# A four-layer graph kernel: two of every sixteen attention units turned on VectorE and carried through memory, a new order of SyncE's loads, and three held chunks in the last layer

## The reference, cut to what matters

```
x = _layernorm(x + _L0_gnn_ref(x, adj, ...))   # agg = adj @ x, then a GRU cell
x = _layernorm(x + _L1_gnn_ref(x, adj, ...))   # D^-1/2 (adj + I) D^-1/2 (x @ W) + b
x = _layernorm(x + _L2_gnn_ref(x, adj, ...))   # 4-head attention over the edges of adj
x = _layernorm(x + _L3_gnn_ref(x, adj, ...))   # hyperbolic layer: support_t = adj @ xt

# the attention
attn  = jnp.einsum('nhc,mhc->hnm', q, k) / np.float32(np.sqrt(C))
e     = jnp.where(mask[None], 0.0, jnp.exp(neg - m))
alpha = e / denom
out   = jnp.einsum('hnm,mhc->hnc', alpha, v)
out   = beta * x_r + (1.0 - beta) * out

# the end of the hyperbolic layer
h  = proj(expmap0(support_t, C_IN), C_IN)
xt = jax.nn.relu(logmap0(h, C_IN))
h  = proj(expmap0(xt, C_OUT), C_OUT)
```

## Time and profile before

| | |
|---|---|
| median of 3 runs | 1879.82 us |
| the profiled execution, its own time | 1879.74 us |
| its span, first to last instruction | 1877.9 us |
| PE busy | 1809.2 us (96%) |
| DVE busy | 1208.7 us (64%) |
| ACT busy | 1023.2 us (54%) |
| POOL busy | 964.4 us (51%) |
| mean granted TensorE clock | 0.985 |

### The profile page before, as it was taken

How to read it: one execution, slowest core, us unless ns; L and a number is a source line. 1 busy time by engine, 2 the same in 40 slices (tenths; PEclk the granted TensorE clock), 3 DMA queues, 4 the chain that set the end, 5 groups by cost and what they waited for, 6 DMA issues and landing times.

```text
span 1877.9 us, 41628 instructions
## 1 busy us (share of the span) xinstructions
PE 1809.2 (96%) x15504; PEld 1217.3 (65%) x15504; DVE 1208.7 (64%) x2246; ACT 1023.2 (54%) x1640; POOL 964.4 (51%) x1069
## 2 busy tenths in 40 slices
PE   7999999999997999999999999999999999889995
PEld 3444444444444888888888888888888888544442
DVE  4777774122226888888889888988889888201111
ACT  0111111000015888888888988888888889213323
POOL 0111111111126657688688787787887886353323
PEclk9999999999997999999999999999999999999998
DMA  9767767899976232313223232233232220879891
GB/s 376 295 229 260 253 230 243 281 385 386 397 267 201 85 91 69 92 57 98 80 75 91 69 92 90 60 92 90 74 90 72 89 77 30 325 238 322 293 319 41
DMA packets 110303, 328.79 MB, mean 175 GB/s; under 512 B 13104, under 2 KB 31280, under 8 KB 85552
## 3 DMA queue, kind: packets, MB, share of 16 engines
q1 hardware_dynamic: 87552, 285.25, 44.2%
q10 hardware_dynamic: 20016, 32.78, 4.8%
q0 software_dynamic: 2560, 8.39, 1.5%
HBM read 299.11 MB, written 27.26 MB: 174 GB/s over the span
## 4 chain that ended last, share of the span: by engine, by line
PE 48%; issue 8%; POOL 7%; ACT 3%; DVE 2%; DMA 1%; POOLq 0%; SPq 0%; DVEq 0%; ACTq 0%
PE bank L562 21%; PE bank L535 13%; PE bank L576 12%; ACT arena L792 2%; POOL arena L1337 1%; POOL small L1337 1%; POOL arena L1330 1%; PE bank L428 1%; DMA arena<-root_dram 1%; DVE arena L1123 1%; POOL small L1276 1%; POOL small L1511 0%; POOL arena L1519 0%; POOL small L1513 0%; POOL small L1496 0%
## 5 line engine op out<-in xcount | busy, mean ns | idle before, releaser
L562 PE MATMUL bank<-ident,arena 128*128 128x128 f32 x4096 | 539.9, 274 | 5.4 <-ACT arena L792 2.4
L562 PEld LDWEIGHTS bank<-ident,arena 128*128 128x128 f32 x4096 | 477.9, 141 | 82.5 <-DVE arena L1123 7.8
L792 ACT ACTIVATE arena<-arena,small 128x2048 f32<-128x2048 f32 x256 | 512.5, 2002 | 0.1
L428 PE MATMUL bank<-arena,stat_s 128*128 128x512 f32 x1016 | 448.5, 599 | 6.9 <-POOL stat_s L1337 4.9
L804 ACT ACTIVATE arena<-bank 128x512 f32<-128x512 f32 x680 | 382.5, 596 | 125.2 <-PE bank L562 123.0
L535 PE MATMUL bank<-k,parts 128*128 128x512 f32 x1024 | 372.0, 445 | 13.9 <-DVE small L1108 6.9
L428 PEld LDWEIGHTS bank<-arena,stat_s 128*128 128x128 f32 x1016 | 193.4, 193 | 237.1 <-issue 230.0
L1123 DVE COPY arena<-bank 128x512 f32<-128x512 f32 x344 | 236.6, 688 | 72.6 <-PE bank L562 71.4
L1330 POOL TENSOR_SCALAR early<-arena 128x512 bf16<-128x512 f32 x128 | 246.2, 1923 | 71.1 <-DVE small L1108 31.4
L576 PE MATMUL bank<-arena,stat_x 128*32 128x128 f32 x8192 | 276.5, 276 | 0.0
L1330 POOL TENSOR_SCALAR arena<-arena 128x512 bf16<-128x512 f32 x128 | 247.1, 1931 | 41.4 <-DVE small L1108 19.6
(11 more groups left out here) (160 smaller groups left out, 1309.3 us busy)
## 6 DMA issues: line engine op xcount, KB each, us to landing
arena<-adj_cols SPq DMA_DIRECT2D x191, 1024.0 KB, 6.0
arena<-adj SPq DMA_DIRECT2D x256, 256.0 KB, 2.7
k_dram<-arena ACTq DMA_DIRECT2D x32, 256.0 KB, 7.1
q_dram<-arena ACTq DMA_DIRECT2D x32, 256.0 KB, 12.2
k<-k_dram POOLq DMA_DIRECT2D x32, 256.0 KB, 8.8
parts<-q_dram SPq DMA_DIRECT2D x128, 64.0 KB, 2.3
x_dram<-arena ACTq DMA_DIRECT2D x16, 256.0 KB, 3.6
arena<-x_dram ACTq DMA_DIRECT2D x16, 256.0 KB, 5.9
```

The costliest lines, as they stand in the source:

```text
L428: mm_ = pe.matmul(bank[:, to, :], stat[:, jt, :], ring[:, s, j, :], start=(jt == 0), stop=(jt == TILES - 1))
L562: last = pe.transpose(bank[:, b_, h * P:(h + 1) * P], cols[:, st % SETS, h, u * P:(u + 1) * P], ident[:, :])
L792: act.activation(cols[:, s_, h, :], cols[:, s_, h, :], ACT.Exp, bias=shift[:, t % 2, 1, i:i + 1], scale=-1.0, accum_out=blocksum[:, t % 2, ...
```

## The change

It has four parts, and nothing else moves.

1. **Two of 16 units are bounced.** `BOUNCED = {11: 1, 15: 6}`: units 11 and 15 of each group have no transposes on PE, no PSUM bank and no copy. DVE turns them at places 1 and 6 of the group in 32x32 blocks into one buffer, `blocks` (four tiles of `stat_s`). SP stores the buffer to memory (256 KB) and loads it back in four transfers of 64 KB into the unit's slot of `turned`. `attend` waits for these and reads the slot through another pattern. DVE copies 32 of the other 112 units and ACT 80; the tables of places change to match.
2. **SP's order.** For each column n of a chunk, SP now loads the mask of column n+7; then, for even n, it stores both units of group n/2, and for odd n loads both. Queries, residuals and the store of `x3` get fixed places between them.
3. **Three held chunks in layer 3** (`HELD` = 3), so that PE has 21 slots to multiply ahead of `xt`. `turn_x3` and `mobius_product` move back by one slot each.
4. **`hyperbolic`** takes no more logarithms. A closed form, `min(un, artanh(MAX_NORM)) / un`, replaces tanh and two logarithms, most of the small steps move from POOL to DVE, and the squares of `relu` run on DVE beside those on ACT.

```diff
+BOUNCED = {11: 1, 15: 6}
+VECTOR_PLACES = (2, 5, 9, 13)
+MASK_AHEAD = 7
...
+            def store_blocks(g):
+                i = block_turns(g)
+                at, before = i % len(BOUNCED), i // len(BOUNCED)
+                sp.wait_ge(blocks_turned, i + 1)
+                if before:
+                    sp.wait_ge(unit_landed[at], 64 * before)
+                sp.dma_start(bounce_dram[at, :, :], blocks).then_inc(blocks_out[at], 16)
+            def load_unit(g):
+                i = block_turns(g)
+                at, before = i % len(BOUNCED), i // len(BOUNCED)
+                sp.wait_ge(blocks_out[at], 16 * (before + 1))
+                sp.wait_ge(unit_used, g - TURNED + 1)
+                for j in range(4):
+                    sp.dma_start(turned[g % TURNED][j * C:(j + 1) * C, :]...,
+                                 bounce_dram[at, :, j * P:(j + 1) * P]...).then_inc(unit_landed[at], 16)
+            def attention_loads(c):
+                for n in range(COLS):
+                    ahead = c * COLS + n + MASK_AHEAD
+                    if ahead < CHUNKS * COLS:
+                        load_mask(ahead // COLS, ahead % COLS, False)
+                    first_unit = c * UPC + n // 2 * UPS
+                    if n % 2 == 0:
+                        for u in BOUNCED:
+                            store_blocks(first_unit + u)
+                    else:
+                        for u in BOUNCED:
+                            load_unit(first_unit + u)
...
+                if is_bounced(k):
+                    i = block_turns(c * UPC + k)
+                    pe.wait_ge(unit_landed[i % len(BOUNCED)], 64 * (i // len(BOUNCED) + 1))
...
+            def turn_blocks(c, k):
+                st, u = k // UPS, k % UPS
+                i = block_turns(c * UPC + k)
+                dve.wait_ge(exp_ready, (c * SPC + st) * H + H)
+                if i > 0:
+                    dve.wait_ge(blocks_out[(i - 1) % len(BOUNCED)], 16 * ((i - 1) // len(BOUNCED) + 1))
+                dve.transpose(blocks..., cols[:, st % SETS, :, u * P:(u + 1) * P]...).then_inc(blocks_turned, 1)
...
-            product(2, 1, {}, to=4, slots=range(SLOTS - 1))
+            product(2, 1, {0: [lambda: mobius_product(last, 3)]}, to=HELD_BANKS[1], slots=range(SLOTS - 1))
+            product(2, 2, {}, to=HELD_BANKS[2], slots=range(SLOTS - 1))
```

More of the change, by code:

```diff
@@ L97, in __call__, with is_bounced, pe_turns, block_turns @@
         return c * len(self.names) + self.names.index(name) + 1
+def is_bounced(k):
+    return k % UPS in BOUNCED
+PE_UNITS = [k for k in range(UPC) if not is_bounced(k)]
+def pe_turns(g):
+    return g // UPC * len(PE_UNITS) + sum(k < g % UPC for k in PE_UNITS)
+def block_turns(g):
+    return g // UPS * len(BOUNCED) + sum(u < g % UPS for u in BOUNCED)
 class TurnBanks:
@@ L108, in __init__ @@
         for k in range(UPC):
-            self.uses.append(("unit", k))
+            if not is_bounced(k):
+                self.uses.append(("unit", k))
             if k % UPT == OUT_AT:
@@ L138 @@
 LAST_BLOCK_CHUNK = CHUNKS - BLOCK // CHUNK
-BY_VECTOR = [k for k in range(UPC) if (k % 16 in VECTOR_PLACES or k in VECTOR_ALSO) and k not in VECTOR_NOT]
-BY_SCALAR = [k for k in range(UPC) if k not in BY_VECTOR]
+BY_VECTOR = [k for k in PE_UNITS if (k % 16 in VECTOR_PLACES or k in VECTOR_ALSO) and k not in VECTOR_NOT]
+BY_SCALAR = [k for k in PE_UNITS if k not in BY_VECTOR]
 EXP_PLACES = [EXP_MOVED.get(k, k) for k in range(1, UPC, 4)]
@@ L351, in load_queries @@
                                  ).then_inc(q4_landed[t % 2], 16)
[L353 to L358, removed]
-                    if m == 5 and not first:
-                        load_residuals(c - 1)
-                    if m == 15 and not first:
+            def store_blocks(g):
[5 more added lines that the diff above has]
+                sp.dma_start(bounce_dram[at, :, :], blocks).then_inc(blocks_out[at], 16)
@@ L408, in _ @@
+            load_slot(HELD, SLOTS - 1, HELD * (SLOTS - 1) + 1)
+            for c in range(HELD + 1, CHUNKS):
+                for s in range(SLOTS):
+                    load_slot(c, s, (c - 1) * SLOTS + s + 1)
             sp.wait_ge(hyp_out, 16 * CHUNKS)
@@ L612, in attention @@
                         scores(*ahead, False)
-                    turn_unit(c, k, first)
+                    if not is_bounced(k):
+                        turn_unit(c, k, first)
                     if k % UPT == OUT_AT:
@@ L1210, in attention @@
                         below_max(c, k // UPT)
+                    for u, place in BOUNCED.items():
+                        if k % UPS == place:
+                            turn_blocks(c, k - place + u)
                     if k in BY_VECTOR:
```

231 lines of the change are left out of this document (127 added, 104 removed).

## The result

The changed kernel took **2083.17 us** (median of 4 runs, 2078.03 to 2086.09) against 1879.87 for the kernel before (1879.78 to 1882.38, 4 runs): a ratio of 1.108, with an interval of 1.106 to 1.110. It is slower, as forecast, by 203 us and not by 150, and it lies 3 us above my range.

What follows compares the result with a forecast made beforehand. PE was taken to bound the attention. Six chunks +168, chunk 0 -2, chunk 7 +6, its end +3 and layer 3 -23 gave +152 on 1879.74: 2032, stated as 2030 us; range 1930 to 2080.

Steps and rivals of the forecast that it cites:

- 32 us a chunk: PE's waits for bounced unit loads: 5.4, 3.9, 8.7, 4.5, 7.3 us in groups 1, 3, 5, 6, 7; about 0.7 in others.
- Inside the same waits: DVE's second transpose, place 6, held some 6 us in groups 5 and 7 by the first's store, within PE's unit-load waits.
- 25 to 35 us a chunk: Sign: PE idle before the attend (L652) for transfers from bounce_dram, 25 to 35 us, largest at place 15, groups 5 and 7.
- DVE's load: In a chunk: eleven copies fewer, sixteen block transposes at 0.69 us more; 113.2 becomes 116.6 us, 127.7 at the upper bound.
- The tail of layer 3: After layer 3's last turn: y written about 8 us later in place of 13.5, a gain of 5.5 us.
- the clock: Half clock on PE after long waits in the attention: 0 to 8 us lost a chunk, 3.5 taken.
- The saving: PE's transposes of two of 16 units gone: 0.47 us a unit, 7.5 us a chunk, 60 us in all.
- 24.5: Net loss of a held chunk before clock: 32 us of waits less 7.5 saved, about 24.5 us more, 152.5 a chunk.
- my 6: Chunk 7: only groups 0 to 4 wait, about 12 us less 7.5, and a little clock: +6 us.
- Chunk 0: First chunk, without post steps: eight waits of 0.7 us against 7.5 saved, -2 us.
- Layer 3: Gain of 23 us (18 from waits and clock, 5.5 from the tail), less 3 for loads queued behind unit loads.
- my 18: PE in layer 3: its waits of 5.62 and 4.88 us and their clock go, -18 us.

Runs made afterwards that it cites:

- e1: The changed kernel with no unit bounced and the earlier tables of places, everything else kept; 1859.46 us, 0.990 of the kernel before.
- e2: The changed kernel with masks loaded 6 columns ahead in place of 7, both units still bounced; 1921.71 us, 1.020 of the kernel before.
- one unit: The changed kernel with only unit 11 bounced, unit 15 turned by PE again; 2052.57 us, 1.092 of the kernel before.
- e13: e11 with ACT's Moebius tanh four places later, at place 95 instead of 91; 1885.18 us, 1.004 of the kernel before.
- e7: No unit bounced, PE's work as in the kernel before; PE waits 4 times a chunk for two small transfers in a row; 1958.25 us.
- e4: The changed kernel with two block buffers for DVE in chunks 0 to 6, SP's order unchanged; 2065.36 us, 1.100 of the kernel before.
- e5: e2 with each mask load issued behind the stores or unit loads of its iteration; 2073.62 us, 1.103 of the kernel before.
- e9: e2 with unit 11's loads issued ahead of the mask load in odd iterations, unit 15's behind it; 1948.20 us, 1.037 of the kernel before.
- e12: e2 with the attention's mask loads (columns from 6 on) issued by ACT in place of SP; 1983.70 us, 1.054 of the kernel before.
- e11: e9 with the block transposes' stores issued by ACT, one place after each transpose, in place of SP; 1896.51 us, 1.009 of the kernel before.
- short pulses: No unit bounced, PE's work as in the kernel before; PE waits 8 times a chunk for one 16 KB transfer; 1925.74 us.

## Why the prediction was right and where it was wrong

**What held.** The direction and the mechanism. Loads behind the queue's wait for POOL are what makes the kernel slow: no bounced units, no loss (e1); one mask column less, 161 us back (e2). The forecast of the **waits** was good: 32 us a chunk plus what PE idles anyway (0.5), against 28.1. "Inside the same waits" for DVE's hold at place 6 is shown by two buffers (18 us less, and the wait moved to the unit loads) and by one unit. Counted by the units that PE attends, the waits of the six chunks came to 4.2, 5.7, 5.4, 4.1 and 8.0 us in groups 1, 3, 5, 6 and 7, for my 5.4, 3.9, 8.7, 4.5 and 7.3.

Their place was not as forecast. "25 to 35 us a chunk" before L652, "largest at place 15 of groups 5 and 7", was 8.1 us a chunk, largest in group 3. In groups 5 and 7 PE waited before scores, for DVE's masks. The lateness is met at DVE first; the sum doesn't mind. DVE's load was read rightly: it came to 115.7 us a chunk, where I said 116.6, and the block transpose took 0.707 us, where I took 0.69. Its group in the page of the profile (count, busy us, mean ns, idle time before it):

```profile
L1191 DVE STREAM_TRANSPOSE stat_s<-arena 128x512 f32<-128x512 f32 x128 | 90.5, 707 | 147.3 <-DMA bounce_dram<-stat_s 145.3
```

The tail of layer 3 fell from 20.2 to 14.6 us, 5.6 for the 5.5 forecast. A 64 KB load landed in 2.2 us and the 256 KB store in 2.2, where I had read 2.3 and 3.4. The section of the Trainium skill that I cited for 2.15 us ("DMA: Bandwidth & Descriptors", "Anatomy of one DMA — SWDGE (gpsimd) path") is on transfers issued by GpSimd, and these are issued by SP; the sum didn't use it.

**The step that failed: the clock.** "With four or five waits of this length a chunk the loss lies between 0 (absorbed in the next wait) and 8 us; I take 3.5." It was 132.5 - 122.1 = 10.4 us a chunk, above my upper bound, and 41 us more over six chunks than the sum had. (122.1 is PE's busy time at full clock with two bounced units, from e13.) I had the price in the earlier trace rows, 1.8 us lost after 4.88 of idleness, 0.37 per us. Then I multiplied it by a count of long waits and took that down by more than half, in place of multiplying it by the idle time of the whole chunk: 0.37 x 28.1 = 10.4. That it fits to the tenth is luck. The long pulses (e7) gave 0.36 with no bounced unit in the program, but the other kernels with two units, against 122.1, give 0.29 to 0.48 for idle times of 10 to 28 us (e2 0.34, e4 0.29, e5 0.34, e9 0.48, e12 0.46), and 0.46 and 0.23 for 8 us (e11, e13).

The Trainium skill ("TensorE: Matmul & The Clock Gate", section "HAM oscillation — how this bites in real kernels") counts the penalty of throttling as half of the throttled time. In the trace, 963.22 us at a mean clock of 0.92 hold 154 us at half clock. The estimate by this page is half of them, 77 us or 12.8 a chunk. The 10.4 measured lie below it; In part of the throttled time PE was idle (from 1202 to 1204 us the clock is 0.50 and PE's busy time nothing), which the page's half doesn't leave out.

**The saving was too large.** My 7.5 us a chunk, 0.47 for each unit, measured 5.4 (e13's chunk at full clock). The earlier trace rows shows a run of transposes with nothing between them. Taken out one by one between scores and attends, a unit brings 0.34 us.

These two, less the waits, are the six chunks: I had 128.05 + 24.5 + 3.5 = 156.05; 4.4 us less of waits, 6.9 more of clock and 2.1 less of saving make 160.6, and 160.5 was measured. That is some 27 of the 51 us that were missing. The way to `x3` of chunk 1 holds 22.8 more, what comes after `x3` of chunk 7 4 fewer (2.0 us for my 6), layer 3 6 more.

**Chunk 0**, the second step that failed, was forecast at -2 us. Up to `x3` of chunk 1 the changed kernel is 20.8 us behind (797.23 for 776.46). Some 11 of them come from a single wait and the half clock behind it:

```profile
568.64 38.31 SPq L372 DMA_DIRECT2D arena<-adj  x12
607.00 4.50 SPq L392 DMA_DIRECT2D bounce_dram<-stat_s  x2
610.43 0.71 DVE L1191 STREAM_TRANSPOSE stat_s<-arena 128x512 f32<-128x512 f32 x1 [9.53 <-DMA bounce_dram<-stat_s]
612.33 1.22 PE L603 MATMUL bank<-k,parts 128*128 128x512 f32 x2 [8.16 <-DVE small L1167]
```

The first store stands behind the loads of six mask columns, which POOL frees one by one until 607. I had costed chunk 0 as a steady chunk without post steps. The rest of the 20.8 is chunk 1, which waits from its first group on.

**Layer 3** gave back 14.0 us (265.8 to 251.8, from the attention's end to the span's), where I summed 20 with the 3 at its start. Without bounced units it was 20.9 (e1). The difference is the new wait of 3.19 us for the first 1 MB, behind the last unit's loads in SP's queue, and the half clock behind it (5.37 us for 8 matmuls where 3.46 is usual): 5.1 us for my 3. Another 2.5 us of PE's stretch are half clock behind the wait of 3.40 us at 1971.25: the 32 matmuls after it take 16.20 us, and 13.90 in e1, where a wait of the same length in the same place cost no clock:

```profile
1749.60 0.66 PE L483 MATMUL bank<-ident,arena 128*128 128x128 f32 x4 [3.40 <-ACT arena L961]
```

In e1, PE's own gain was 15.8 us for my 18: this wait was not foreseen.

**The version to keep** is e1: the new layer 3 and SP's order without bounced units, 0.990 of the kernel before.

## What to carry to other kernels

A wait in a queue that several engines share couples them. Before a transfer is put into such a queue, ask of every wait ahead of it whose progress it follows, and of everything behind it who will wait for it: here either order closed a circle through POOL, DVE and PE, and moving the mask loads to the queue of a busy engine only moved it. When a forecast has PE waiting, price the clock on all of its idle time and not on the few longest waits, and as a range: 0.23 to 0.48 us per us in these kernels, 0.36 with the long pulses, 0.17 where more than half of the idle time was in waits of up to 1.5 us. And a saving read from a row where an instruction stands in a run is an upper bound for one taken out of a mixed stretch.

## What was not expected of the hardware

- Half clock came after waits as short as 2.20 us (long pulses) and 2.23 us (short pulses), and not after one of 3.32 us (short pulses). In layer 3 a wait of 3.40 us was followed by it in the changed kernel and not in e1. The length of a wait alone didn't decide it here.
- With short pulses, most of them of 0.6 to 1.5 us, a chunk ran at a mean granted clock of 0.98 to 1.00, although PE idled for some 6% of it.
- Which queue issues a store mattered, its own speed didn't: the stores landed in 2.6 us (median) both from SP's queue (e9) and from ScalarE's (e11), and the kernel with ScalarE's was 52 us faster.
